# A recurrence step on one core: the first low product split into two halves of the output channels

## What is computed

```python
x = x + _L0_cond_ref(x, cond, base_layer, w1, b1, w2, b2, ln_g, ln_b)   # the first layer
xW = jnp.einsum('ntd,dh->nth', x, Wx) + b
def step(prev_h, xw):
    next_h = jnp.tanh(prev_h @ Wh + xw)
    return (next_h, next_h)
_, h_t = jax.lax.scan(step, h0, xW_t)       # 1024 steps, h is (2, 256)
x = x + h_t
```

## Time and profile before

| | us |
|---|---|
| median of 3 runs | 777.74 (777.73 to 778.85) |
| the profiled execution's own time | 778.8 |
| its span | 776.6 |
| PE busy, products | 695.0 (89%), 18801 of them |
| PE busy, weight loads | 626.7 (81%) |
| ACT busy | 501.1 (65%) |
| DVE busy | 305.5 (39%) |
| POOL busy | 6.4 (1%) |

### The profile page before, as it was taken

The page is one execution under the profiler, slowest core; times in us unless marked ns, Lnnn a source line. Parts: engine busy times, 40 slices in busy tenths (PEclk is TensorE's granted clock), DMA queues, the critical chain, the costliest instruction groups (busy, mean ns, idle before and its releaser), DMA issues.

```text
span 776.6 us, 45957 instructions
## 1 busy us (share of the span) xinstructions
PE 695.0 (89%) x18801; PEld 626.7 (81%) x18801; DVE 305.5 (39%) x1539; ACT 501.1 (65%) x5140; POOL 6.4 (1%) x18
## 2 busy tenths in 40 slices
PE   5699999999999999999999999999999999999987
PEld 4588888888888888888888888888888888888886
DVE  6633443333434333434333334333443333334332
ACT  6366666666666666666666666666666666666665
POOL 3000000000000000000000000000000000000000
DMA  8000000000000000000000000000000000000000
GB/s 274 10 5 10 11 9 11 11 6 10 11 11 8 11 8 9 11 11 8 11 7 9 11 11 9 11 7 8 11 11 9 11 6 9 11 11 9 7 7 6
DMA packets 12285, 12.36 MB, mean 16 GB/s; under 512 B 1813, under 2 KB 11056, under 8 KB 12080
## 3 DMA queue, kind: packets, MB, share of 16 engines
q1 hardware_dynamic: 11984, 9.45, 4.3%
q0 software_dynamic: 96, 0.02, 0.0%
HBM read 7.36 MB, written 2.10 MB: 12 GB/s over the span
## 4 chain that ended last, share of the span: by engine, by line
PE 70%; ACT 19%; DVE 5%; issue 3%; DMA 1%; SPq 1%; DVEq 0%; another core or an unknown queue 0%
PE acc L321 46%; ACT h_pre L447 17%; PE pre L321 14%; PE p_w L285 4%; PE pre L301 4%; DVE x_s L521 3%; PE p_w L280 2%; DMA w_f<-w_dram 1%; DVE x_f L520 1%; ACT p_f L453 1%; DVE h_lo L567 1%; PE pre L298 1%; SPq L219 0%; ACT h_rnd L455 0%; ACT w_s L493 0%
## 5 line engine op out<-in xcount | busy, mean ns | idle before, releaser
L321 PE MATMUL acc<-h_pre,wh_s 128*128 128x2 f16 x8192 | 385.0, 168 | 54.8 <-DVE acc L562 0.6
L447 ACT ACTIVATE h_pre<-pre 128x2 f16<-128x2 f32 x2046 | 240.7, 170 | 251.5 <-PE pre L321 251.5
L321 PEld LDWEIGHTS acc<-h_pre,wh_s 128*128 128x128 f16 x8192 | 302.1, 106 | 115.6 <-ACT h_pre L447 99.6
L567 DVE TENSOR_TENSOR h_lo<-p_f,h_pre 128x4 f16<-128x4 f32 x1024 | 173.0, 169 | 450.2 <-ACT p_f L453 450.0
L321 PE MATMUL pre<-h_rnd,wh_s 128*128 128x2 f16 x4092 | 270.6, 170 | 3.7 <-issue 0.2
L321 PE MATMUL acc<-h_lo,wh_s 128*128 128x2 f16 x4096 | 258.5, 167 | 4.6 <-DVE h_lo L567 0.5
L321 PEld LDWEIGHTS pre<-h_rnd,wh_s 128*128 128x128 f16 x4092 | 190.8, 108 | 6.3 <-ACT h_rnd L455 6.0
L321 PEld LDWEIGHTS acc<-h_lo,wh_s 128*128 128x128 f16 x4096 | 188.5, 106 | 7.1 <-DVE h_lo L567 7.1
L457 ACT ACTIVATE h_f<-acc 128x4 f32<-128x4 f32 x1024 | 186.4, 182 | 0.5 <-PE acc L321 0.5
L455 ACT ACTIVATE h_rnd<-acc 128x4 f16<-128x4 f32 x1022 | 172.8, 169 | 0.0
L453 ACT ACTIVATE p_f<-acc 128x4 f32<-128x4 f32 x1023 | 161.6, 158 | 7.2 <-PE acc L321 7.2
(11 more groups left out here) (76 smaller groups left out, 150.0 us busy)
## 6 DMA issues: line engine op xcount, KB each, us to landing
w_f<-w_dram SPq DMA_DIRECT2D x8, 512.0 KB, 9.1
x_in<-x_dram SPq DMA_DIRECT2D x32, 64.0 KB, 2.3
out_dram<-o_row SPq DMA_DIRECT2D x64, 32.0 KB, 1.9
w_f<-w_dram SPq DMA_DIRECT2D x1, 256.0 KB, 2.9
base_f<-base_dram SPq DMA_DIRECT2D x1, 256.0 KB, 11.4
wh_f<-wh_dram SPq DMA_DIRECT2D x1, 256.0 KB, 11.0
wx_f<-wx_dram SPq DMA_DIRECT2D x1, 256.0 KB, 11.0
cond_r<-cond_dram SPq DMA_DIRECT2D x1, 2.0 KB
```

The source lines that it names most:

```text
L321: return nc.tensor.matmul(dst, wh_s[:, pw, ki, mo * P:(mo + 1) * P], h[:, par, ki, :], start=False, stop=True, skip_group_check=True)
L447: nc.scalar.activation(h_pre[:, n % 2, m, :], src, func, scale=scale).then_inc(s_hpre[(n // HALF) % 2], 1)
L567: nc.vector.tensor_sub(h_lo[:, par].rearrange("p m b -> p (m b)"), p_f[:, 0:COLS], h_pre[:, par].rearrange("p m b -> p (m b)")).then_inc(s ...
```

## The change

The first of the four low products, output half 0 and input half 0, is done as two products. Each has all 128 rows of input channels, and 64 columns of weights, so 64 output channels. The first writes partitions 0 to 63 of the output, the second 64 to 127. The other three low products are as before. The two halves are issued in the place of the first product, behind the wait for h_lo.

```diff
                 pe.wait_ge(s_hlo[half], u + 1)
-                for mo, ki in TILES:
+                for side in range(2):
+                    rows = slice(side * P // 2, (side + 1) * P // 2)
+                    nc.tensor.matmul(full[rows, 0, :], wh_s[:, 0, 0, rows], h_lo[:, par, 0, :], start=False, stop=True,
+                                     skip_group_check=True)
+                for mo, ki in TILES[1:]:
                     done = onto(full[:, mo, :], 0, mo, ki, h_lo)
                 done.then_inc(s_sum[half], 1)
```

## The result

The changed kernel takes 979.18 us (median of 4 runs, 978.68 to 979.89) against 778.28 us for the kernel before on the same chips: a ratio of 1.258 (95% interval 1.256 to 1.260), slower. The forecast was 808 with a range of 800 to 880. The direction was right and the size was not: the step from one p_f to the next grew by 0.207 us, where the sum had 0.031.

A forecast was written before the change was run, and what follows sets the result against it. The bound was taken as step latency in one serial loop of 1024 steps, mostly PE. 24 + 7 = +31 ns a step, 31.7 us, less 1.9 given back, on 778.8 gave 808.6, stated as 808 us; range 800 to 880.

The forecast's parts named there:

- The bound: Whole kernel: one serial loop of 1024 steps; a nanosecond added in the low group is 1.02 us in the kernel.
- Nothing else ends later: In a step: only the chain p_f, h_lo, low products counts; h_rnd's four products add no readable wait to it.
- (a), the first half load: At the head of the low group: a 64-column load takes 128 ns against 104, +24 ns a step.
- (b), the second half load: Right after the first half load: runs beside it and adds 7 ns; 54 if it runs behind it.
- (c): Three full low products behind the halves: they keep their pace of 27 ns, +0.
- A rule that speaks against this change: Trainium skill: changing tiling mode drains the engine; at output transpose L280 the trace shows a switch costing at most some 10 ns.
- The rival of the drain: At switches around the halves: +0.16 us each, 1016 us with one, 1178 with both; chance 0.13 for 880 to 1178.
- Behind each other (855): Rival at the second half load: it adds 54 ns, so 78 ns a step and 855 us; chance 0.33.
- Two ordinary products (805): Rival at the halves: run as ordinary products, one pace of 27 ns more, 805 us; counted within the forecast's range.
- not slower (765): Rival at the first low load: half as long, last low product 13 ns sooner, 765 us; chance 0.06, half of it faster.
- (d), given back: In 31 blocks, where DVE is the bound: two p_f intervals swallow the extra, 31 x (31 + 31) ns = 1.9 us back.
- (e), the fillers at nothing: Behind the low group: at most seven fillers, 190 ns, with 0.06 us of cover, of which the change takes 0.03; no cost.

The follow-up runs named there:

- split_last: Against the kernel before: the three full low products come first, the first low product follows them as two halves of 64 columns; 904.04 us.
- split_hpre: Against the kernel before: the first of the eight h_pre products is done as two 64-column halves, instead of the first low one; 885.45 us.

## Why the prediction was wrong, point by point

**The bound** was right: one serial step, p_f to p_f, and every nanosecond in the low group is 1.02 us. "Nothing else ends later" did not hold for the changed kernel. There h_lo is ready 0.14 ahead of the halves' load, and what the load waits for is the end of the h_rnd products. PE's lines for pre went from 14% to 25% of the chain and h_rnd from 0% to 5%. The two had been close before: the first low load stands 0.03 behind the last h_rnd load, one pace of the queue.

**(a), the first half load,** was right as the length of the load: 128 at the median against 104, +24.

**(b), the second half load,** was right: the halves run side by side, with two loads in the time of one. It was taken as 7 ns; leaving one half out gives back 6 ns a step, whichever half it is. The inference from row groups (L417) to column groups held.

**(c) is where the sum failed.** "The three full products behind keep their pace of 27: +0" took no account of a gap behind the halves: 0.14 instead of 0.03. And no term at all stood for the gap ahead of them, 0.09. Both were put at nothing in "A rule that speaks against this change", by the step "So a switch costs at most some 10 ns there", carried from L280 to the halves. L280 is a product in transpose mode, and the two runs in which the same output is turned without that mode have the gaps in full. The row was read correctly, but it showed no change of form: the f32 transpose goes with the full products, and has the gap only where divided products stand beside it (split_last, split_hpre). I had written that L280 "is a transpose" as the reason why the drain kept a chance, and gave it 0.13 with everything above 880; the plain reading of the Trainium skill's rule was the right one.

**The rival of the drain** was the mechanism that came true, with its price off. It put each change of form at 0.16, until the recorded end of the product ahead; the loads start 0.07 before that end. The gap ahead cost 0.085. From the first low load to p_f it was 0.122 more, in which the narrow load, the gap behind and the slower start of the full products are contained. The rival also had the halves behind each other. So the step grew by 0.207 and the time is 979 us, below both of its cases (1016 with one drain, 1178 with both), though both drains are there. It is outside the range, which left both out. The rival's last sentence, a shorter gap anywhere above 808, covers it without a price.

**Behind each other (855)** fell with the loads of 0.13 for two and with the pairs of 0.053. **Two ordinary products (805)** and **not slower (765)** fell with the time, the second also with a half load of 0.128. By its own sum the range ends at 881 or 882 instead of 880; nothing hangs on that.

**(d), given back,** was right in mechanism: the steps in which DVE was the bound now run at the plain step's pace. "1.00 whatever PE does" was not right. That interval is 0.92 now, since the first cast x_s starts 0.31 ahead of its p_f (420.47, 420.78), where it had started 0.09 ahead (407.02, 407.11), and holds h_lo up for less. So 10 us came back, where its rule would give 31 x (0.207 + 0.04) = 7.7 for a step longer by 0.207.

**(e), the fillers at nothing,** held in the changed kernel: a step with six fillers (402.36 to 403.28) is as long as a plain one (421.70 to 422.62), 0.92.

On the rule of the Trainium skill (TensorEngine Tiling (Array Packing), Key Properties) that changing the tiling mode drains the engine: the traces agree for products outside transpose mode, for 64 columns, 32 columns and 64 rows, in that the load behind the change waits until 0.07 ahead of the end of the product before it. The output transpose (L280, f32, 64 columns) does not contradict it, as I had taken it to: it behaves as a product of the undivided array. The Trainium skill's other rule there, that different tiles load and multiply in parallel, is borne out for columns by the two loads in 0.13 and the four in 0.11.

## What to carry to other kernels

A product that uses half of the array's rows or columns, put between full ones, cost two pauses here besides its own time: the load behind each change waited until 0.07 us before the product ahead ended. In this chain of short products that made 0.2 us a step, where a full product takes 0.027 of the queue. Three things made it cheaper. Eight halves in one group cost no more than two (0.907 against 0.920). A place where PE waits anyway halved the cost. A width that leaves the array undivided had no pause (96 columns, 51 ns). The full product was cheaper than any of them.

Before a price is carried over from a row, check that the row has the same mode. An instruction that looks alike by shape may stand on the other side of the change, and the test is which neighbours it has a gap with.

## What was not expected of the hardware

- An f32 transpose with 64 columns has no gap towards full products on either side, and has one towards plain products of 64 columns; the same shape as a plain product, f32 or f16, has the gap towards full products.
- The load behind a change starts 0.071 to 0.073 us ahead of the recorded end of the product ahead, for products that last 0.165 to 0.42 us.
- Loads of 32, 64 and 96 f16 columns take 0.10, 0.128 and 0.155 us, one of 128 takes 0.104: the load of the full width is shorter than those of 64 and 96 columns.
- A plain f32 product of 64 columns stands with two loads and two products where transpose mode has one of each, and takes 0.69 instead of 0.41 us.
- The loads of four column groups start within 0.01 us of each other, and the four cost no more than two.
